# A causal attention's row maxima: one masked addition for both heads' diagonal blocks and a plain maximum, in place of a fused add-and-maximum for each head and query chunk

## What is computed

```python
def _mla(h, Wq, Wdkv, Wuk, Wuv, Wo):          # 16 heads of 8 features
    q = (h @ Wq).reshape(B, S, HEADS, hd)
    c = h @ Wdkv
    k = (c @ Wuk).reshape(B, S, HEADS, hd)
    v = (c @ Wuv).reshape(B, S, HEADS, hd)
    scores = jnp.einsum('bqhd,bkhd->bhqk', q, k) / jnp.sqrt(jnp.asarray(hd, h.dtype))
    causal = jnp.tril(jnp.ones((S, S), bool))
    scores = jnp.where(causal, scores, jnp.asarray(-1000000000.0, h.dtype))
    a = jax.nn.softmax(scores, axis=-1)
    out = jnp.einsum('bhqk,bkhd->bqhd', a, v).reshape(B, S, D)
    return out @ Wo
```

## Time and profile before

| | |
|---|---|
| median of 3 runs | 653.47 us (652.43 to 654.01) |
| span of the profiled execution | 653.3 us |
| that execution's own time | not given apart; its span lies within the runs |
| PE busy | 623.2 us (95%), 4941 instructions |
| DVE busy | 514.0 us (79%), 1901 |
| ACT busy | 408.9 us (63%), 747 |
| POOL busy | 251.8 us (39%), 319 |
| fused add-and-maximum, line 1330 | 512 instructions, 128 each over 128, 256, 384 and 512 elements |
| mean granted clock of PE | 0.977 of 2.4 GHz |

### The profile page before, as it was taken

One profiled execution on the slowest core, in us unless ns is written; L12 is line 12 of the kernel. 1 busy time (PEld: TensorE's weight loads), 2 busy tenths in 40 slices (PEclk: granted clock), 3 DMA queues, 4 the chain that ended last, 5 costly groups with the idle time before them and its releaser, 6 DMA issues. The chain is left out here.

```text
span 653.3 us, 14269 instructions
## 1 busy us (share of the span) xinstructions
PE 623.2 (95%) x4941; PEld 409.0 (63%) x4941; DVE 514.0 (79%) x1901; ACT 408.9 (63%) x747; POOL 251.8 (39%) x319
## 2 busy tenths in 40 slices
PE   7999899999899999999999999999999999999996
PEld 3576544454466666676666666766666666666885
DVE  3756967957778899888898889878978888873666
ACT  3563446575667576867686668666867566755443
POOL 8130422322423365335334533353334333543442
PEclk9999969899899999999999999999999999999999
DMA  8700000000000000000000000000000000000000
GB/s 306 224 12 24 1 4 2 2 2 3 3 2 3 3 3 3 9 11 3 3 18 3 3 3 3 19 2 3 15 7 2 3 18 3 2 3 18 1 17 17
DMA packets 15192, 12.69 MB, mean 19 GB/s; under 512 B 6729, under 2 KB 13330, under 8 KB 14866
## 3 DMA queue, kind: packets, MB, share of 16 engines
q1 hardware_dynamic: 14370, 11.78, 5.8%
q10 hardware_dynamic: 752, 0.01, 0.1%
HBM read 9.16 MB, written 2.10 MB: 17 GB/s over the span
## 5 line engine op out<-in xcount | busy, mean ns | idle before, releaser
L1240 ACT ACTIVATE prob<-psW 128x1024 f32<-128x1024 f32 (+1 forms) x192 | 183.2, 954 | 107.7 <-PE psW L1106 107.2
L1330 DVE CUSTOM_DVE_ANT_0 psS<-psS,maskb 128x128 f32<-128x128 f32 (+1 forms) x498 | 231.9, 517 | 22.1 <-PE psS L1088 19.6
L917 POOL TENSOR_SCALAR_AFFINE_SELECT prob<-prob 128x512 f32<-128x512 f32 x128 | 80.0, 635 | 218.3 <-ACT prob L1240 218.3
L1064 PE MATMUL turn<-wexp,late 128*128 128x128 f32 x1016 | 126.5, 278 | 0.4 <-DVE late L1394 0.4
L1064 PEld LDWEIGHTS turn<-wexp,late 128*128 128x128 f32 x1016 | 118.9, 192 | 5.7 <-issue 3.6
L1202 ACT ACTIVATE late<-turn 128x512 f32<-128x512 f32 x128 | 76.3, 597 | 62.5 <-PE turn L1056 53.1
L1394 DVE SCALAR_TENSOR_TENSOR late<-late,turn 128x512 f32<-128x512 f32 x128 | 87.2, 682 | 33.4 <-ACT late L1202 32.6
L1088 PE MATMUL psS<-kT,qT 24*128 24x256 f32 (+1 forms) x498 | 106.2, 412 | 4.9 <-DVE top L1330 4.7
L1106 PE MATMUL psW<-qT,kT 26*128 26x256 f32 (+2 forms) x512 | 94.1, 404 | 6.9 <-ACT prob L1240 6.7
L928 POOL TENSOR_TENSOR late<-late 128x512 f32<-128x512 f32 x62 | 79.8, 1288 | 53.5 <-DVE late L1423 46.9
L1118 PE MATMUL psV<-prob,va 128*32 128x512 f32 (+3 forms) x1024 | 91.0, 450 | 0.4 <-POOL prob L917 0.4
(11 more groups left out here) (273 smaller groups left out, 848.1 us busy)
## 6 DMA issues: line engine op xcount, KB each, us to landing
qT<-shiftT SPq DMA_DIRECT2D x256, 2.0 KB
prob<-in_xT SPq DMA_DIRECT2D x4, 512.0 KB, 6.5
X<-in_x SPq DMA_DIRECT2D x1, 2048.0 KB, 16.1
out<-late SPq DMA_DIRECT2D x8, 256.0 KB, 2.4
prob<-in_wqkvT SPq DMA_DIRECT2D x1, 1024.0 KB
late<-in_w SPq DMA_DIRECT2D x1, 1024.0 KB, 10.5
prob<-in_wqkvT SPq DMA_DIRECT2D x2, 256.0 KB, 3.7
late<-in_woutT SPq DMA_DIRECT2D x1, 512.0 KB
```

The costliest lines, as they stand in the source:

```text
L917: pool.affine_select(out=blk, in_=blk, compare_op=ALU.is_ge, fill=0.0, base=0, pattern=[[0, 4], [1, P]], channel_multiplier=-1).then_inc(s ...
L1064: last = mm(into[:, D * c:D * c + D], hid[:, n % 2, k, P * c:P * c + P], wexp2[:, n, k, :], start=(k == 0), stop=(k == 1))
L1240: A(into, src, ACT.Exp).then_inc(s["exp_ready"], 1)
L1330: last = V.tensor_tensor_reduce(at, at, maskb[:, T - P * (c + 1):T], 1.0, BIG, ALU.add, ALU.max, top[:, u % 2, c, 2 * p + j:2 * p + j + 1])
```

## The change

It replaces, in each of the 192 `maximum` steps, the fused instructions and accumulator reads by one addition of the triangle to the diagonal blocks of both heads, and one maximum for each query chunk over both heads. The maxima wait for the addition (the `own` chain's semaphore). `s_ps` and `max_ready` now count whole steps: PE waits until both banks are done before it writes either, and DVE starts when all of a step's scores are there. The score matmuls read `qT[..., u % 4, ...]`, the group's own queries. The counts in `shift` and in the first `weight` step follow.

```diff
--- before.py
+++ after.py
@@ -1077,19 +1077,15 @@
                     if i == 0:
                         wait_free(pe, "queries", b, g)
                         wait_free(pe, "keys", b, g)
-                    used = 2 * scores_used(b, n)
-                    wait(pe, "max_ready", used - 1)
+                    wait(pe, "max_ready", scores_used(b, n))
                     for i, c in enumerate(cs):
                         keys = max(P * (c + 1), HALF)
                         for j in range(2):
-                            if used > 0 and i == 0 and j == 1:
-                                pe.wait_ge(s["max_ready"], used)
                             row = R * (2 * p + j)
                             last = mm(scores_in(b, n)[:, j, HALF * i:HALF * i + keys],
-                                      qT[row:row + SHIFT, u % 2, P * c:P * c + P], kT[row:row + SHIFT, g, 0:keys],
+                                      qT[row:row + SHIFT, u % 4, P * c:P * c + P], kT[row:row + SHIFT, g, 0:keys],
                                       start=True, stop=True, tile_position=(row, 0))
-                            if i == len(cs) - 1:
-                                last.then_inc(s["s_ps"], 1)
+                    last.then_inc(s["s_ps"], 1)
                 elif what == "weight":
                     g, i = divmod(n, WEIGHT_STEPS)
                     u = NG * b + g
@@ -1097,7 +1093,7 @@
                     if i == 0:
                         pe.wait_ge(shift_in[u % 2], 16 * SHIFT_MOVES * (u // 2 + 1))
                     if u == 0 and i == 0:
-                        wait(pe, "max_ready", 2 * AHEAD)
+                        wait(pe, "max_ready", AHEAD)
                     wait(pe, "exp_ready", WEIGHT_STEPS * u + i)
                     for i, kc in enumerate(kcs):
                         q0 = min(P * kc, HALF)
@@ -1323,16 +1319,18 @@
                     u = NG * b + g
                     cs, p = SCORES[i]
                     step = SCORE_STEPS * u + i
-                    for j in range(2):
-                        dve.wait_ge(s["s_ps"], 2 * step + j + 1)
-                        for i, c in enumerate(cs):
-                            at = scores_in(b, n)[:, j, HALF * i:HALF * i + P * (c + 1)]
-                            last = V.tensor_tensor_reduce(at, at, maskb[:, T - P * (c + 1):T], 1.0,
-                                                          BIG, ALU.add, ALU.max, top[:, u % 2, c, 2 * p + j:2 * p + j + 1])
-                        last.then_inc(s["max_ready"], 1)
+                    dve.wait_ge(s["s_ps"], step + 1)
+                    blocks = scores_in(b, n)[:, :, :].rearrange("p j (x t) -> p j x t", t=P)
+                    diagonal = blocks[:, :, 0:C:3, :] if len(cs) == 2 else blocks[:, :, cs[0]:cs[0] + 1, :]
+                    triangle = maskb[:, T - P:T].unsqueeze(1).unsqueeze(1).broadcast_to([P, 2, len(cs), P])
+                    own(V.tensor_tensor(diagonal, diagonal, triangle, ALU.add))
+                    for i, c in enumerate(cs):
+                        last = V.tensor_reduce(top[:, u % 2, c, 2 * p:2 * p + 2],
+                                               scores_in(b, n)[:, :, HALF * i:HALF * i + P * (c + 1)], AX, ALU.max)
+                    last.then_inc(s["max_ready"], 1)
                 elif what == "shift":
                     u = NG * b + n
-                    dve.wait_ge(s["max_ready"], 2 * SCORE_STEPS * (u + 1))
+                    dve.wait_ge(s["max_ready"], SCORE_STEPS * (u + 1))
                     if u >= 2:
                         dve.wait_ge(shift_in[u % 2], 16 * SHIFT_MOVES * (u // 2))
                     parts = shift[:, u % 2, :].rearrange("p (i h c) -> p c h i", i=2, c=C)
```

## The result

| | before | after |
|---|---|---|
| median | 653.74 us (4 runs, 652.43 to 660.3) | 703.10 us (4 runs, 699.96 to 706.51) |
| ratio | 1 | 1.0719, 95% interval 1.0665 to 1.0773 |
| span of the profiled execution | 653.3 us | 703.7 us |
| mean granted clock of PE | 0.977 | 0.94 |

A forecast was written before the change was run, and what follows sets the result against it. PE was taken as the bound from 188 to 577 us, DVE having 13% left. 653.3 us plus 31 there plus 10 from 70 to 188 us gave 694 us; forecast 670 to 706 us (chance 0.70), wider range 666 to 716.

The forecast's parts named there:

- The price of a step: DVE's maxima steps: 1.65, 1.32, 1.59 us for 1.22, 1.00, 1.26; a group 9.12 against 6.96, 69 us over 32 groups.
- Rival 2: Maxima steps: reads cost DVE 0.14 us each, so it gains 0.9 us a group; about 646 us, chance 0.06.
- The idle time that goes: 188 to 577 us: of DVE's 52.3 us idle, 11 and 12 stay, 8 come; with 52 of work, 31 us longer.
- waits for the tanh: 188 to 577 us, before a `gate`: all 20.0 us go, as DVE comes 0.3 to 0.4 us later in every slot.
- because PE issued `hidden` before it was stopped: 188 to 577 us: reason given why DVE's 20.0 us of waiting before a `gate` would go.
- The joint hand-over: 188 to 577 us: PE writes scores only when both heads are done, so DVE waits for them; 8 us.
- The early part: 70 to 188 us, 8 groups: DVE gets 17 us; 4 land directly, half of the other 13; 10 us, between 3 and 17.
- Idle time swallowing it: Rival, 70 to 577 us: DVE's 52.3 us idle takes the 52 us of work; 653 to 668 us, chance 0.11.
- Faster: Rival 2: maxima steps get cheaper by records and PE regains 4.7 to 12.7 us of waits; about 646 us, chance 0.06.
- All of it landing: Rival 3's first half: waits on both sides stay over 70 to 577 us, 52 + 17 us; 722 us, shared chance 0.13.
- rival 3: All added work lands (722 us), or PE's clock falls too, with part of the waits (706 to 730 us); chance 0.13.
- Other signs: Expected, 188 us to maxima's end: DVE above 92%, PE below 94%; weight-load waits several times 12.7 us; batch 69 to 70 us.

The follow-up runs named there:

- The extra work alone: One unread DVE reduction of 256 mask elements added at the start of each maxima step, against the kernel before: 692.91 us, ratio 1.0545.

## Why the prediction was right

**The mechanism** was right: DVE's elements go from 5120 to 7168 a group, DVE had about as much idle time as it got work, and the two engines in a fixed order can't use it up. The extra work alone, on the kernel before, gives 5.5% of the 7.2%. The total was forecast 9 us short, inside the range; several terms of the sum were off, some against each other, so that the sum came this close is partly luck.

**The price of a step.** "A group's 9.12 us" was right: 1.66 and 1.60 us measured for 1.65 and 1.59. "Against 6.96" was too low. I took steps of the kernel before that are followed by an instruction that may start early. Where a waiting one follows, the accumulator's read lasts to its end and costs its 0.14 us, as in this step of chunk 3 in the kernel before:

```profile
334.19 0.69 DVE L1330 CUSTOM_DVE_ANT_0 psS<-psS,maskb 128x512 f32<-128x512 f32 x1
...
335.44 0.14 DVE L1330 DVE_READ_ACCUMULATOR2_ANT top<- 128x1 f32 x1
335.62 0.18 DVE L1340 TENSOR_SCALAR shift<-top 128x16 fp32r<-128x16 f32 x1
```

That is 1.39 us (to 335.58), not 1.26, and of the 48 steps of chunk 3 in the late part about 30 were of this kind, of chunk 2 too. Summed over the late part's steps, DVE spent 177.5 us before and 225.3 after (each step from its start to the next instruction's, or to its own end if that comes first): 48 us more, where I had 52. Rival 2 had this much truth in it, and no more: the read is free only when the next instruction waits for nothing.

**The idle time that goes.** This is the step that failed. I let the 20.0 us of waits for the tanh vanish and 9 of the 20.2 for `down`, put 8 for the scores and kept 12 of smaller idle times: 31 us. Measured are 13.1, 18.6, 5.2 and 5.6: 42.5 us, and 4.9 of gaps behind the additions, which I had counted as work. Two `gate`s of a batch show why the tanh waits did not vanish, each before and with the change:

```profile
376.58 0.69 DVE L1394 SCALAR_TENSOR_TENSOR late<-late,turn 128x512 f32<-128x512 f32 x1 [0.92 <-ACT late L1202]
```

```profile
407.81 0.69 DVE L1392 SCALAR_TENSOR_TENSOR late<-late,turn 128x512 f32<-128x512 f32 x1 [0.56 <-ACT late L1198]
```

```profile
400.20 0.69 DVE L1394 SCALAR_TENSOR_TENSOR late<-late,turn 128x512 f32<-128x512 f32 x1 [0.79 <-ACT late L1202]
```

```profile
429.90 0.18 PEld L1085 LDWEIGHTS psS<-kT,qT 24*128 24x128 f32 x2 [0.32 <-DVE top L1328]
...
434.29 0.69 DVE L1392 SCALAR_TENSOR_TENSOR late<-late,turn 128x512 f32<-128x512 f32 x1 [0.73 <-ACT late L1198]
```

Most of these waits were 0.7 to 0.9 us long, and a longer step of maxima can take away only what it adds. Twenty-five `gate`s of the late part wait in both kernels. At 20 of them the wait fell by 0.30 us on average, as at the first pair: no more than the 0.3 to 0.4 us that I had named myself, where "vanish" asks for all of it. At the other five, as at the second pair, it did not fall, and there the score step ahead of the unit had waited some 0.3 us for the maxima. So "because PE issued `hidden` before it was stopped" does not hold at these five, where the unit stands behind a score step that was stopped, and the size was wrong at the 20. Of the 27 waits with the change, 20 have no such stop of PE in the 3.5 us ahead of the unit.

The joint hand-over, for which I charged 8 us and which alone costs 0.3, costs 6.7 late once DVE is loaded. In the kernel before, head 0's scores went out 0.6 us ahead of the rest; with the change PE waits at such places for both heads, up to 1.22 us late in the kernel.

The late part adds up so: the steps 48 us more (forecast 52), the rest of DVE's busy time 4 less (forecast none), the idle time outside the steps 10 less (forecast 21). That is 34 us, where I had 31: the errors cancel in good part.

**The early part** was sized at 10 us, with half of its work hidden in 28.7 us of idle time. From the pair of profiles 16.3 us came, all of the work (15.8 us by the steps); from the other executions between 8 and 16, 12 on average. DVE's waits for scores stayed (19.4 us, 19.6 before), although half of the work was to go into them. That they can't hide the maxima, since PE may not write scores before these are done, is an argument from the order of the steps; it was not tried by itself.

**The rivals.** Idle time swallowing it: refuted; DVE's idle time fell by 5 us in 52, or by 10 without the gaps behind the additions. Faster: refuted as a forecast of this change, for the reads cost a part of their time only. The advice against fusing and for fewer instructions (the Trainium skill, VectorE: DVE Perf Modes, section Rules for kernel authors) did not pay here: with 14 instructions in a group in place of 16 and their 16 reads, but 7168 elements in place of 5120, the kernel is 7.2% slower, a part of it by the joint hand-over. All of it landing: not in the late part (34 us for 48 of longer steps); early it may have. The clock falling late came true in small (0.98; 3.4 us), so by the prediction's own sign, a PEclk below 1.00 after 200 us, rival 3 had a share, though the time stayed under its 706 to 730 us. Other signs were missed too: DVE is busy 89% of the late part, not above 92%; PE 96%, not below 94%; the weight loads' waits went from 12.7 to 31.7 us, two and a half times; two thirds of the waits for the tanh stayed; and a batch takes 70.6 us, not 69 to 70. The rule that a semaphore between DVE instructions costs nothing extra (the Trainium skill, VectorE: DVE Perf Modes, section The DRAIN you can't avoid) would have had the maximum start as early as one that waits for nothing. The trace disagrees: behind the addition of 0.69 us it starts 0.72 us after (438.48), where an instruction with nothing to wait for starts 0.08 us before the end. That is 5 us of gaps in the late part, and 0.08 us of lost overlap in each step beside them.

How much of DVE's work lands depends on how full it already is. Late part, 24 groups:

| kernel | DVE busy | late part | of the step from the row above |
|---|---|---|---|
| unmasked, both heads at once | 309.2 | 380.5 | |
| unmasked, by head | 321.6 | 383.1 | 21% |
| before | 336.7 | 389.1 | 40% |
| after | 375.9 | 423.4 | 88% |
| addition twice | 450.4 | 493.8 | 94% |

The rows differ in the hand-over too: the second and third hand over by head, the others jointly. The extra work alone, by head, has 377.1 and 416.9 us, 69% of its step from "before": the rise from 40% stands without the joint hand-over, and the 88% includes it. In the last row the clock is lower as well.

## What to carry to other kernels

A fused instruction that masks and compares in one pass is hard to beat by two instructions that go over some of the data twice, even if they are fewer: count elements out of PSUM, and measure a step from one start to the next, in places with a waiting and with a free successor. If the slower engine has as much idle time as the change adds, do not expect it to be used: compare each single wait with what the change adds ahead of it, since a wait of 0.8 us shrinks only by the 0.3 us that come, and ask what stands behind the instruction of the other engine that now waits longer. And a mask before a maximum that only shifts a softmax can be left out where no masked score lies far above the allowed ones of its row: that gave 2.2% (1.4 to 2.9).

## What the runs showed of the hardware that was not expected

- The accumulator read behind a fused instruction is free if the next instruction waits for nothing and costs its 0.14 us if the next one waits: 1.22 to 1.26 us against 1.36 to 1.39 for the same step.
- A joint hand-over costs nothing on a DVE that is busy 87% of the time (0.3 us in 389) and 1.6% on one that is busy 90% (416.9 to 423.5 us).
- Behind a single wait of PE of 1.2 us, in a window of 10 us in which PE was busy for 8.7 to 8.8 us, the granted clock of the window fell to 0.83 at three places, that is, for a part of it PE ran at the lower level (1.2 GHz), and stayed at 1.00 at two (275 to 285 and 485 to 495 us); with three unread matmuls in the gap it stayed at 1.00 at all of them. The late part moved by 3.4 us in 423.
- The late part of this program repeats within 0.3 us across executions (389.07 and 389.07, with the address of the queries alone between them; 423.42 and 423.18), while the early one, with the same instructions, took 118.4 and 123.9 us, and 134.7 and 131.6, at clocks of 0.88 and 0.85, 0.78 and 0.82. Between these profiled executions the spread lies there; what in it starts the difference was not tried.
